# A decoder block with routed experts: float16 halves of the expert matrices replaced by plain float32

## The reference

```python
x = layernorm(x + self_attention(x))          # 16 heads, a linear bias on the keys, bias on q, k, v, out
x = layernorm(x + cross_attention(ctx, x))    # 16 heads, masked keys
logits = x_flat @ gate_w.T                    # 4096 tokens, 8 experts
probs = softmax(logits); topk_probs, topk_idx = top_k(probs, 2)
hidden = relu(einsum('th,ehf->tef', x_flat, w1) + b1)      # w1: (8, 256, 1024)
all_out = einsum('tef,efh->teh', hidden, w2) + b2          # w2: (8, 1024, 256)
y = sum over the two chosen experts of all_out * topk_probs
x = layernorm(x + y)
```

## Time and profile before

| | |
|---|---|
| three runs | 1415.9, 1416.11, 1416.43 us; median 1416.11 |
| the profiled execution | 1412.27 us, of which the span from first to last instruction is 1410.2 us |
| mean granted TensorE clock | 0.906 |
| TensorE matmul busy | 1091.7 us, 77% of the span |
| VectorE busy | 1022.0 us, 72% |
| ScalarE busy | 567.4 us, 40% |
| POOL busy | 483.5 us, 34% |
| DMA | 202.20 MB, mean 143 GB/s |

### The profile page before, as it was taken

One profiled execution on the slowest core, in us unless ns is written; L12 is line 12 of the kernel. 1 busy time (PEld: TensorE's weight loads), 2 busy tenths in 40 slices (PEclk: granted clock), 3 DMA queues, 4 the chain that ended last, 5 costly groups with the idle time before them and its releaser, 6 DMA issues. The chain is left out here.

```text
span 1410.2 us, 32514 instructions
## 1 busy us (share of the span) xinstructions
PE 1091.7 (77%) x9874; PEld 772.1 (55%) x9875; DVE 1022.0 (72%) x2410; ACT 567.4 (40%) x1022; POOL 483.5 (34%) x597
## 2 busy tenths in 40 slices
PE   3778899889888888888885600088999999999980
PEld 2445666666655655565553400066777777777750
DVE  2579999999888989999985340066777777777764
ACT  1344555555545656665563200022323323332324
POOL 1233433433344343534322037612223223223324
PEclk7799999999999999999997555599999999999995
DMA  8489886678756887788754152275222222222227
GB/s 207 108 225 226 230 200 142 157 180 227 174 108 163 235 237 154 207 232 221 202 168 137 68 194 106 100 267 159 42 43 43 41 45 41 41 45 41 43 30 245
DMA packets 160383, 202.20 MB, mean 143 GB/s; under 512 B 30444, under 2 KB 141692, under 8 KB 157067
## 3 DMA queue, kind: packets, MB, share of 16 engines
q1 hardware_dynamic: 145864, 182.92, 48.7%
q0 software_dynamic: 13296, 17.83, 7.5%
q10 hardware_dynamic: 1152, 0.53, 0.2%
HBM read 122.63 MB, written 74.41 MB: 140 GB/s over the span
## 5 line engine op out<-in xcount | busy, mean ns | idle before, releaser
L1177 PE MATMUL HB<-xhi,W 128*128 128x128 f16 x2272 | 292.1, 221 | 21.7 <-issue 16.1
L1177 PEld LDWEIGHTS HB<-xhi,W 128*128 x2272 | 202.2, 98 | 65.8 <-issue 48.2
L1177 PE MATMUL HB<-xlo,W 128*128 128x128 f16 x1136 | 225.0, 220 | 0.0
L1460 POOL DMA_INDIRECT d_sums<-ysc,tok x71 | 111.0, 1563 | 327.3 <-DMA XB<-d_rows 171.7
L892 ACT ACTIVATE PT<-SB 128x1024 f32<-128x1024 f32 x128 | 131.1, 1024 | 138.3 <-PE SB L563 136.3
L659 DVE TENSOR_REDUCE mneg<-SA 128x4 f32<-128x1024 f32 x128 | 156.5, 1223 | 41.6 <-PE SA L515 39.5
L1177 PEld LDWEIGHTS HB<-xlo,W 128*128 x1136 | 111.9, 99 | 50.2 <-issue 0.7
L1370 DVE SCALAR_TENSOR_TENSOR hlo<-HB,hhi 128x512 f16<-128x512 f32 x142 | 98.2, 691 | 55.1 <-ACT hhi L1238 51.1
L1238 ACT ACTIVATE hhi<-HB 128x512 f16<-128x512 f32 x142 | 84.2, 593 | 121.3 <-DVE HB L1362 121.2
L1362 DVE SCALAR_TENSOR_TENSOR HB<-HB,SC,b1c 128x512 f32<-128x512 f32 x142 | 107.1, 754 | 16.7 <-PE HB L1177 11.9
L1246 ACT ACTIVATE ysc<-yb,wv 128x256 f32<-128x256 f32 x71 | 36.1, 508 | 191.8 <-DVE yb L1394 181.6
(11 more groups left out here) (195 smaller groups left out, 2500.4 us busy)
## 6 DMA issues: line engine op xcount, KB each, us to landing
wst<-in_w SPq DMA_DIRECT2D x32, 1024.0 KB, 10.0
d_w<-w SPq DMA_DIRECT2D x16, 1024.0 KB, 6.7
W<-d_w SPq DMA_DIRECT2D x8, 2048.0 KB, 8.7
k_stack<-d_k SPq DMA_DIRECT2D x96, 128.0 KB, 7.2
XB<-d_rows SPq DMA_DIRECT2D x71, 130.0 KB
d_rows<-fill SPq DMA_DIRECT2D x4, 1950.0 KB, 15.6
d_q<-q_part SPq DMA_DIRECT2D x16, 384.0 KB, 5.8
d_k<-k_part SPq DMA_DIRECT2D x16, 384.0 KB, 2.7
```

Of the source, the lines that this page charges most:

```text
L1177: mm = pe.matmul(out, w.rearrange("p e n -> p (e n)"), x[n % 2][:, k, :], start=(k == 0 and half == 0 and x is xhi), stop=(k == KT - 1 and ...
L1460: pool.indirect_dma_start(YS, bass.IndirectOffsetOnAxis(ap=tok[n % 6][:, 0:1], axis=0), ysc[n % 2][:, :], None, compute_op=ALU.add).then_i ...
```

## The change

The experts are computed in plain float32. The float16 tile `W` and the memory `d_w` go. The second matrices of all eight experts stay on chip as float32 (`W2`, 64 KB a partition), two of them loaded before the first block and the others one each in the first six. The first matrix is loaded anew for every block, from the input, into one of three buffers (`W1`, 1 MB a load), two blocks ahead. A block has then 16 float32 matmuls of 128 columns and 8 of 256 in place of 48 float16 ones of 128, 8 of 256 and 8 of 512. The halves of inputs and hidden rows go, with their VectorE operations, and so do the scales; the bias is added by a plain addition. In attention all modes go: no reductions, no scales, no halving, no loads and stores of expert matrices; the loop over the middle iterations is one of eleven. The padding fills move from iterations 6 and 7 to 14 and 15.

```diff
     def iterations(step, eng, chain=None, per=0):
-        step(-1, None)
-        for i in (0, 1, 2):
-            step(i, "max")
-        looped(step, eng, 3, 6, "max", chain, per)
...
+        with eng.Fori(3, B - 2) as i:
...
-    FILL_STEPS = (0, 1, 2, 6, 7)
+    FILL_STEPS = (0, 1, 2, B - 2, B - 1)
...
-            ins = dve.tensor_reduce(wmx[:, k, c, bass.ds(i, 1)], wst[k][:, c * QW:(c + 1) * QW], AX.X, ALU.max,
-                                    apply_absolute_value=True)
...
-            ins = dve.scalar_tensor_tensor(half_of(k, 1, c), quarter(k, c), SC[:, k:k + 1], half_of(k, 0, c),
-                                           ALU.mult, ALU.subtract)
...
-            act.activation(half_of(k, 0, c), quarter(k, c), ACT.Copy, scale=SC[:, k:k + 1]
-                           ).then_inc(sem(f"whi{k}"), 1)
...
-    W = sb("W", [P, NE, 2, 2, WC], F16)
+    W1 = [sb(f"W1_{k}", [P, KT, F]) for k in range(3)]
+    W2 = sb("W2", [P, NE, FT, D])
...
+        def load_second(e):
+            if e:
+                sp.wait_ge(sem("ld_W2"), 16 * e)
+            sp.dma_start(W2[:, e], ap["w2"][e].rearrange("(a p) n -> p a n", p=P)).then_inc(sem("ld_W2"), 16)
+
+        def load_first(j, n):
+            e = sp.value_load(BEi[0:1, bass.ds(j, 1)], min_val=0, max_val=NE - 1)
+            sp.dma_start(W1[n % 3][:, :, :], ap["w1"][bass.ds(e, 1)].rearrange("e (a p) n -> p (e a) n", p=P)
+                         ).then_inc(sem(f"ld_W1_{n % 3}"), 16)
...
             load_rows(j + 2, n % 2)
+            if not (isinstance(j, int) and j < 1):
+                wait(sp, "HB", 2 * j)
+            load_first(j + 2, n + 2)
             if isinstance(j, int) and j < HEAD:
-                load_weights(NE - HEAD + j)
+                load_second(NE - HEAD + j)
...
+        def first_in(j, n):
+
+            if isinstance(j, int):
+                return 16 * (j // 3 + 1)
+            return 16 * (ROUND // 3 * turn_of["m"] + n // 3 + 1)
...
             for k in range(KT):
-                for half, x in ((0, xhi), (0, xlo), (1, xhi)):
-                    w = W[:, bass.ds(e, 1), 0, half, k * F + f * P:k * F + (f + 1) * P]
-                    mm = pe.matmul(out, w.rearrange("p e n -> p (e n)"), x[n % 2][:, k, :],
-                                   start=(k == 0 and half == 0 and x is xhi), stop=(k == KT - 1 and half == 1))
+                mm = pe.matmul(out, W1[n % 3][:, k, f * P:(f + 1) * P], xt[n % 2][:, k, :],
+                               start=(k == 0), stop=(k == KT - 1))
...
-            if f > 0:
-                pe.matmul(YP[n % 2][:, 0:D], hlo[n % 3][:, f, :], w[:, 0:D], start=False, stop=False)
-            mm = pe.matmul(YP[n % 2][:, :], hhi[n % 3][:, f, :], w, start=(f == 0), stop=(f == FT - 1))
+            w = W2[:, bass.ds(e, 1), f].rearrange("p e n -> p (e n)")
+            mm = pe.matmul(YP[n % 2][:, 0:D], hid[n % 3][:, f, :], w, start=(f == 0), stop=(f == FT - 1))
...
             if now:
-                pe.wait_ge(sem("ld_W"), 16 * e + 16)
-                wait(pe, "xlo", j + 1)
+                wait(pe, f"ld_W1_{n % 3}", first_in(j, n))
+                wait(pe, "xt", j + 1)
             if before:
-                wait(pe, "hlo", 2 * (j - 1))
+                pe.wait_ge(sem("ld_W2"), 16 * e2 + 16)
+                wait(pe, "relu", 2 * (j - 1))
...
-            dve.scalar_tensor_tensor(bank, bank, SC[:, 3:4],
-                                     b1c[:, bass.ds(e, 1), 4 * c:4 * c + 4].rearrange("p e f -> p (e f)")
-                                     .unsqueeze(2).to_broadcast([P, 4, P]), ALU.mult, ALU.add
-                                     ).then_inc(sem("hid"), 1)
+            dve.tensor_tensor(bank, bank, b1c[:, bass.ds(e, 1), 4 * c:4 * c + 4].rearrange("p e f -> p (e f)")
+                              .unsqueeze(2).to_broadcast([P, 4, P]), ALU.add).then_inc(sem("hid"), 1)
...
-            chain(dve.scalar_tensor_tensor(yl[:, :], YP[n % 2][:, D:2 * D], SC[:, 4:5],
-                                           b2r[:, bass.ds(e, 1), :].rearrange("p e d -> p (e d)"),
-                                           ALU.mult, ALU.add))
-            dve.scalar_tensor_tensor(yb[:, :], YP[n % 2][:, 0:D], SC[:, 4:5], yl[:, :],
-                                     ALU.mult, ALU.add).then_inc(sem("yb"), 1)
+            dve.tensor_tensor(yb[:, :], YP[n % 2][:, 0:D], b2r[:, bass.ds(e, 1), :].rearrange("p e d -> p (e d)"),
+                              ALU.add).then_inc(sem("yb"), 1)
```

More of the change, by code:

```diff
@@ L223, in iterations @@
     def iterations(step, eng, chain=None, per=0):
-        step(-1, None)
-        for i in (0, 1, 2):
-            step(i, "max")
-        looped(step, eng, 3, 6, "max", chain, per)
-        step(6, "max")
-        step(7, "max")
-        step(8, "scale")
-        step(9, "halve")
-        looped(step, eng, 10, B - 2, "halve", chain, per)
-        step(B - 2, "halve")
-        step(B - 1, "halve")
-        step(B, "halve")
-        step(B + 1, None)
-    def looped(step, eng, first, end, mode, chain, per):
+        for i in (-1, 0, 1, 2):
+            step(i)
         n = chain.n if chain else 0
-        with eng.Fori(first, end) as i:
+        with eng.Fori(3, B - 2) as i:
             if chain:
-                chain.n, chain.count = n + per * (i - first), 0
-            step(i, mode)
+                chain.n, chain.count = n + per * (i - 3), 0
+            step(i)
             assert not chain or chain.count == per, chain.count
         if chain:
-            chain.n = n + per * (end - first)
+            chain.n = n + per * (B - 5)
+        for i in (B - 2, B - 1, B, B + 1):
+            step(i)
     def group(u, i, back):
@@ L388, in step @@
                 later_loads()
-            experts_out(i - 1, mode, 0)
-            if mode == "scale":
-                wait(sp, "wmax0", NE)
-                experts_in(i, "halve", 0)
-            elif not (isinstance(i, int) and i in (7, B)):
-                experts_in(i, mode, 0)
             if on(i):
@@ L414, in _ @@
         sp.wait_ge(sem("wr_fill"), 16 * (len(FILL_STEPS) + 1))
-        for k in range(2):
-            sp.wait_ge(sem(f"wr_w{k}"), 16 * NE)
     @block.tensor
@@ L609, in gap, with step @@
                 item(name, i + off, i)
-        def step(i, mode):
+        def step(i):
             for u in range(2 * NG):
@@ L800, in step @@
-        def step(i, mode):
+        def step(i):
             for u in range(2 * NG):
-                if mode == "scale" and u == 0:
-                    greatest()
-                if mode == "scale" and u == 3:
-                    scales()
                 if u < NG:
@@ L1156, in turn @@
             wait(pe, "ld_XB", 16 * (j + 1))
-            wait(pe, "xlo", j)
+            wait(pe, "xt", j)
             for k in range(KT):
@@ L1217, in step, with round_starts @@
                     second(n - 2, e2, f)
-        blocks(step, pe, start=lambda m: packed(pe, m, found))
+        def round_starts(m):
+            turn_of["m"] = m
+            packed(pe, m, found)
+        blocks(step, pe, start=round_starts)
     @block.scalar
@@ L1379, in weights @@
             wait(dve, "ld_XB", 16 * (j + 1))
+            wait(dve, "wv", j)
             of = BEf[:, bass.ds(j, 1)]
@@ L1409, in step @@
                 hidden(j, n, e, 0)
-            if not (fixed and j >= NBLK - 1):
-                xhalf(j + 1, n + 1)
             if now:
-                low(j, n, 0)
                 hidden(j, n, e, 1)
-                low(j, n, 1)
-        blocks(step, dve, chain, 2, lambda m: packed(dve, m, found))
+        blocks(step, dve, chain, 1, lambda m: packed(dve, m, found))
         def moments(s):
```

153 lines of the change are left out of this document (23 added, 130 removed).

## The result

The changed kernel takes 1446.12 us (median of 4 runs, 1442.91 to 1451.11), the kernel before in the same session 1416.01 (4 runs, 1412.02 to 1416.43). The ratio is 1.0222, 95% interval 1.0187 to 1.0258: slower, by 30 us and not by the 81 predicted (whether by more than 2%, the interval leaves open). The profiled execution took 1442.91 us (span 1441.1) against 1412.27 (span 1410.2): +30.6.

What follows compares the result with a forecast made beforehand. TensorE was taken to set the expert blocks' pace, with VectorE not attention's bound. Attention -33.4 and experts +114.7 gave +81.3 on 1412.27, 1493.6; with 3.8 for the median, 1497 us, range 1474 to 1520.

Steps and rivals of the forecast that it cites:

- The 0.92 us beside the steps stay: Expert blocks: turning matmuls, block restart and loop turn keep costing 0.92 us a block, unknown +-0.2; block +1.74 us.
- head: Turn of expert block 0 to turn of block 7: +1.3 us, up to +8 if the load backlog is not covered.
- drain: End of the expert blocks, after block 70's turn: +3.8 us, from longer matmuls less one VectorE operation.
- TensorE's float32 time sets the blocks: Likeliest case, expert blocks; attention gains little: 1497 us, chance 0.80, own range 1478 to 1514.
- the step: One of eight in an expert block: four float32 matmuls at 0.111 us and two at 0.217, 0.878 us against 0.66.
- Rival 4: Expert blocks: float32 weight loads not hidden beside matmuls, 3.5 us more a block, +250, about 1745 us; chance 0.01.
- rival 5: Expert blocks: float32 matmuls run as one instruction each, step 0.44 us, adds set 4.8 us a block, -91; chance 0.02.
- the stream is hidden: Expert blocks: the 1 MB load a block takes 4.4 us of a 7.9 us period, issued two blocks ahead, so hidden.
- rival 3: Expert blocks: output adds, each waiting for the one before, become the bound: +26, 1523 us; chance 0.09.
- rival 2: Attention: VectorE was the bound, iteration falls to 37.9 us, -105, 1421 us; chance 0.03 (half-way case 1464, 0.05).
- The attention iteration: Attention: 42.9 us an iteration, bounds 40.7 to 43.3; 15 iterations save 29.4 us, range -62 to -23.
- The 0.26 us read from iteration 8: Attention: second half of iteration 8, without four reductions, ran 0.26 us shorter than iteration 5's; taken as the second-half gain.

Runs made afterwards that it cites:

- one reordering: Kernel before with the first matrix's float16 halves streamed, and VectorE's three small row-weight operations moved ahead of the last low-half subtraction: 1375.78 us, ratio 0.9731.
- the two edits above: Kernel before, first product always reading expert 0's halves at a fixed address, and VectorE's hidden low half taken of 4 elements, not 512: 1386.35 us, ratio 0.9796.

## Why the prediction was wrong in size

**The step that failed** is "The 0.92 us beside the steps stay". It was taken over as a constant, with +-0.2 for computed addresses and waits, and only 0.21 us of it (the turning matmuls) was TensorE's own work. The other 0.71 was time in which TensorE's sequencer, and right behind it VectorE, held up a TensorE that needs only 5.5 us for its float16 matmuls. A longer matmul does not add to such time, it covers it. By the prediction's own terms the block should have been 8 x 0.878 + 0.21 = 7.23, against 7.245 measured, and the run would have been forecast at 1497 - 63 x 0.71 = 1452 us. The trace of before had the hint: a gap of about 1.2 us for "issue" at every loop turn, while TensorE was called the engine that sets the pace. The busy share hid most of the rest: a matmul's record lasts longer than the time to the next start, so only 19.6 of the 394 us showed as idle, where 45 were lost. This one term made 46.9 of the 50.7 us between 1493.6 and 1442.91. The other terms missed by +4.8 us (attention), -4.0 (head) and -3.9 (drain), and that they come to only 3.8 in all is in part luck.

**Right:**
- That TensorE's float32 time sets the blocks, and the step: 0.88 us from halves 0.11 and 0.22 us apart. Rival 4 (loads not hidden) and rival 5 (one instruction each) are refuted by it. The page gives x2272 matmuls of the first product, two for each of the 16 written ones in 71 blocks. The rule of the Trainium skill ("TensorE: Matmul & The Clock Gate", Part 3, The mechanism) weighed under rival 4 stays at odds with the trace: loads of 192 ns stand beside matmuls 0.11 us apart (four in 1104.22 to 1104.66), and no step is longer for them.
- That the stream is hidden: 5.0 us a load (page, median), TensorE without a wait for it.
- That the adds do not become the bound (rival 3): they landed in 5.3 us at the median with the stream on, 5.8 at most, against a period of 7.245, and none waited for the one before (by source, 1000 to 1300 us):

```profile
DMA to landing us min/median/max: 4.4/5.3/5.8
```

- That VectorE's work in the first half of attention was not its bound (rival 2 refuted): with the reductions gone VectorE idles in front of the maxima, for TensorE's scores. Groups by line, after, 300 to 600 us:

```profile
L591 DVE TENSOR_REDUCE mneg<-SA 128x4 f32<-128x1024 f32 x56 | 68.6, 1225 | 23.2 <-PE SA L447 23.2
```

**Off in size:**
- The attention iteration, 43.35 us where 42.9 was taken. The 0.26 us read from iteration 8 were not a gain from four missing reductions: putting eight back moved nothing. Of the 24.6 us gained, 6.6 are the scales' iteration (49.9 to 43.36) and 19.8 the seven with subtractions and copies (319.99 to 300.20); the first seven, which had reductions, took 304.69 where they had taken 302.95. Scaled copies cost nothing; the subtractions alone do.
- The head, -2.7 where +1.3 was taken: it holds blocks to which the same constant was applied (five of 7.1 to 7.9; they took 5.09 and four times 7.25). That the same step failed there is argued from this; no run took it apart.
- The drain, -0.1 where +3.8 was. There the path was wrong: TensorE's last matmul did move, from 15.0 to 17.9 us behind the turn of block 70, but the last three adds end the chain. They wait for each other, 4.4 to 4.6 us apart (1368.76, 1373.18 and 1377.72 before; 1399.66, 1404.25 and 1408.84 after), and the last starts 22.6 and 22.7 us behind that turn. The first of the three starts no later than before (13.7 and 13.5 us).

**Left open:** how the 0.71 us divide between sequencer and VectorE in the kernel before, since each hides the other; the runs give only nothing for VectorE, 0.19 for the addresses and 0.47 us for both, the last with 1.4 us still lost at each loop turn (0.23 us a block, by estimate), which is read from the trace as VectorE's sequencer. Whether a float32 block would also cover 40 addresses was not run. Also whether the subtraction's further cost comes through POOL's longer operations or through VectorE's longer copies.

## What to carry to other kernels

Before a constant of a period is carried over to a changed kernel, ask which engine makes it: what lies between TensorE's matmuls is covered by longer matmuls and comes back with shorter ones. When an engine is nearly always busy and still has gaps for "issue", count the computed addresses and loop turns of its sequencer, and look how close the next engine's period is: two bounds 0.2 us apart give little or nothing one at a time. A change with two parts should be timed in parts: here the streaming won 16 us, with one reordering 40, and the float32 matmuls took 73 us more than the streamed float16 ones (456.4 against 383.0 from turn 7 to turn 70).

## What the hardware showed beyond what was expected

- A computed address costs TensorE's sequencer 0.124 us, start to start, though its record is 46 ns long; with five of them for eight float16 matmuls that take 0.66 us, the sequencer becomes the bound, and it shows at the start of a block (0.40 us) more than within it. The turn of the hardware loop costs 1.2 us of idle TensorE in the kernel before, and none in the kernel after.
- The same turn leaves VectorE idle for 0.83 and 0.85 us in the kernel before; with the two edits above it holds TensorE for 1.4 us.
- A float16-writing subtraction of 512 columns on VectorE with two inputs on chip lengthened VectorE's `q_stack` copy from 0.65 to 0.92 us and POOL's `k_rest` from 1.16 to 1.67; a reduction of the same length and one input lengthened neither.
- Indirect adds landed in 3.8 us alone, in 5.3 with 1 MB loads every 7.25 us, in 4.3 to 4.8 with 1 MB loads every 5.8 to 6.1 us.
